# Macaron layer in fp32r on one core: x loaded one chunk ahead in the projections, and the first score maxima spread differently over their steps

## The reference

```
x = x + 0.5 * ffn(layernorm(x))
x = x + attention(layernorm(x))          # 16 heads of 32
x = x + 0.5 * ffn(layernorm(x))          # the same ffn weights

ffn(y)       = relu(y @ sign(up).T * up_scale) @ sign(down).T * down_scale * output_scale   # 2048 hidden
attention(y) = softmax(q k.T / sqrt(32)) v @ w_o.T,   q, k, v = y @ w_q.T, y @ w_k.T, y @ w_v.T
```

## Time and profile before

| | |
|---|---|
| median of 3 runs | 3113.91 us (3111.85 to 3114.26) |
| the profiled execution | 3113.91 us, span 3112.0 us |
| mean granted clock of TensorE | 0.986 |
| TensorE busy | 2973.2 us, 96% of the span |
| VectorE, ScalarE, GpSimd busy | 65%, 52%, 43% |
| projection stage | about 511 to 861 us of the span |

### The profile page before, as it was taken

How to read it: one execution, slowest core, us unless ns; L and a number is a source line. 1 busy time by engine, 2 the same in 40 slices (tenths; PEclk the granted TensorE clock), 3 DMA queues, 4 the chain that set the end, 5 groups by cost and what they waited for, 6 DMA issues and landing times.

```text
span 3112.0 us, 38839 instructions
## 1 busy us (share of the span) xinstructions
PE 2973.2 (96%) x14768; PEld 1964.9 (63%) x14768; DVE 2038.0 (65%) x3044; ACT 1613.9 (52%) x2851; POOL 1331.3 (43%) x489
## 2 busy tenths in 40 slices
PE   6999999998799999999999999999999889999998
PEld 4888887876555555555555555555555447888887
DVE  4555556766587777777787777787877234555552
ACT  5344443322166666666666666666666553333333
POOL 0000000000078787878787878788888700000000
PEclk9999999999899999999999999999999989999999
DMA  4110012563287888888888787878787754222200
GB/s 141 62 55 28 28 55 88 186 214 119 84 203 170 192 179 195 177 192 177 190 177 193 174 197 172 200 173 197 178 194 181 192 148 120 57 55 54 55 28 28
DMA packets 184891, 428.54 MB, mean 138 GB/s; under 512 B 89728, under 2 KB 90752, under 8 KB 148224
## 3 DMA queue, kind: packets, MB, share of 16 engines
q0 software_dynamic: 32400, 235.94, 32.7%
q1 hardware_dynamic: 152304, 190.11, 22.0%
HBM read 121.91 MB, written 67.63 MB: 61 GB/s over the span
## 4 chain that ended last, share of the span: by engine, by line
PE 71%; ACT 9%; DMA 6%; DVE 5%; POOL 4%; issue 4%; SPq 0%; ACTq 0%; POOLq 0%; DVEq 0%
PE bank L426 15%; PE bank L445 15%; PE bank L830 12%; PE bank L802 9%; PE bank L553 8%; ACT att_p L786 8%; PE bank L806 6%; DMA att_dma_acc<-att_p 5%; POOL att_acc L710 4%; PE bank L317 3%; DVE att_row_max L737 2%; PE bank L851 2%; PE bank L846 1%; DVE norm_inv L108 1%; ACT head_total L228 0%
## 5 line engine op out<-in xcount | busy, mean ns | idle before, releaser
L737 DVE TENSOR_REDUCE att_row_max<-bank 128x1 f32<-128x512 f32 x2048 | 1258.5, 683 | 383.5 <-PE bank L806 379.9
L786 ACT ACTIVATE att_p<-bank 128x512 f32<-128x512 f32 x2048 | 1047.0, 620 | 585.2 <-PE bank L802 573.2
L710 POOL TENSOR_TENSOR att_acc<-att_acc,att_p 128x2048 f32<-128x2048 f32 x217 | 993.4, 4578 | 222.9 <-ACT att_p L786 218.4
L802 PE MATMUL bank<-att_q,att_k 98*128 98x512 f32 x2048 | 852.7, 418 | 30.2 <-ACT att_p L786 25.6
L806 PE MATMUL bank<-att_k,att_q 96*128 96x512 f32 x2048 | 815.9, 400 | 48.8 <-DVE att_row_max L737 38.0
L802 PEld LDWEIGHTS bank<-att_q,att_k 98*128 98x128 f32 x2048 | 385.9, 189 | 403.1 <-issue 210.2
L830 PE MATMUL bank<-att_p,att_v 128*32 128x512 f32 x4096 | 502.1, 608 | 0.0
L806 PEld LDWEIGHTS bank<-att_k,att_q 96*128 96x128 f32 x2048 | 390.5, 191 | 123.6 <-DVE att_row_max L737 45.3
L369 DVE TENSOR_TENSOR ffn_hid_lo<-ffn_hid,ffn_hid_hi 128x512 fp32r<-128x512 f32 x256 | 176.1, 688 | 430.7 <-ACT ffn_hid_hi L404 412.8
L401 ACT ACTIVATE ffn_hid<-bank,up_s 128x512 f32<-128x512 f32 x256 | 176.1, 688 | 474.8 <-PE bank L426 474.2
L426 PE MATMUL bank<-hi,ffn_up_w 128*128 128x512 f32 x1024 | 402.7, 393 | 20.3 <-DVE lo L122 15.3
(11 more groups left out here) (89 smaller groups left out, 2215.9 us busy)
## 6 DMA issues: line engine op xcount, KB each, us to landing
att_dma_acc<-att_p POOLq DMA_DIRECT2D x225, 1024.0 KB, 7.6
x<-x_after_ffn SPq DMA_DIRECT2D x16, 1024.0 KB, 7.4
att_q<-q_hi SPq DMA_DIRECT2D x64, 256.0 KB, 4.2
att_k<-k_hi SPq DMA_DIRECT2D x64, 256.0 KB, 8.9
x<-xT SPq DMA_DIRECT2D x8, 1024.0 KB, 7.1
x_after_ffn<-x_out SPq DMA_DIRECT2D x8, 1024.0 KB, 9.3
q_hi<-qkv_o_hi SPq DMA_DIRECT2D x32, 256.0 KB, 2.0
q_lo<-qkv_o_lo SPq DMA_DIRECT2D x32, 256.0 KB, 2.5
```

What stands on the lines that cost most here:

```text
L710: self.nc.gpsimd.tensor_tensor(self.acc[H % 2][:], a[:], self.prob[kt % PR][:], ALU.add).then_inc(self.summed, 1)
L737: self.nc.vector.tensor_reduce(self.row_max[odd][:, qt, q:q + 1], m[:], axis=AX.X, op=ALU.max).then_inc(self.m_read, 1)
L786: self.nc.scalar.activation(self.prob[kt % PR][:, q * CH:(q + 1) * CH], self.s_ps[S_BANK[kt * QC + q]][:], ACT.Exp, scale=SCALE).then_inc( ...
L802: self.nc.tensor.matmul(self.s_ps[S_BANK[i]][:], self.k_st[H % NB][0:KM, kt * P:(kt + 1) * P], self.q_st[H % NB][0:KM, q * CH:(q + 1) * CH ...
```

## The change

It has two parts, both in the projection stage. In the steps' table, chunk 4 carries two maxima in each of steps 4 to 11 (before: steps 8 to 11), and chunks 5 and 6 one in every step (before: two in steps 0, 3, 6 and 9, one in the others). The total stays at 80, and chunk 7 keeps its 40. In SyncE's list, x of chunk n + 1 is loaded at the head of chunk n, for n from 1 to 6, where x of chunk n + 2 was loaded at the head of chunk n, for n from 0 to 5. The wait ahead of the load keeps its form.

```
-FIRST_AT = {**{(4, t): 2 for t in range(8, NT)}, **{(n, t): 1 if t % 3 else 2 for n in (5, 6) for t in range(NT)},
+FIRST_AT = {**{(4, t): 2 for t in range(4, NT)}, **{(n, t): 1 for n in (5, 6) for t in range(NT)},
             **{(7, t): 4 for t in (0, 1, 2, 3, 4, 5, 8, 9, 10, 11)}}
...
                 for n in range(NCH):
-                    if n < NCH - 2:
+                    if 1 <= n < NCH - 1:
                         sp.wait_ge(norm.dve, NV * (NCH + n + 1))
-                        st.load(sp, NCH + n + 2, x1)
+                        st.load(sp, NCH + n + 1, x1)
                     for t in range(NT):
                         qkv.store(sp, n, t)
```

## The result

| | before | after |
|---|---|---|
| median | 3113.21 us (3111.85 to 3114.26, 4 runs) | 3158.32 us (3157.16 to 3158.67, 4 runs) |
| ratio, 95% interval | | 1.0144 (1.0127 to 1.0163) |
| the profiled execution | 3113.91 us, span 3112.0 | 3161.7 us, span 3159.7 |
| projections, from chunk 1 on | 309.6 us | 352.8 us |

A forecast was written before the change was run, and what follows sets the result against it. TensorE, busy 96% of the span, was taken as the bound. Chunks 1 to 3 +22.0, chunk 4 +17.65 and +8.8, chunks 5 and 6 -5.7 sum to +42.8 us on 3113.91: 3156.7, range 3146 to 3169.

The forecast's parts named there:

- chunks 1 to 3: Projections: each chunk pays an x wait of 5.65 us and 1.7 us of lower clock, +22.0 us in all.
- chunk 4: Projections: first maximum 17.65 us later, x wait included, and +8.8 us from there to the chunk's end.
- chunks 5 and 6: Projections, twelve maxima each: 3.75 us wait goes, 4.1 us of the 6.87 stay; -2.15 and -3.55, together -5.7 us.
- The x wait: TensorE ahead of the mean product, waiting for late x: 5.65 us in chunks 1 to 4, 5.4 in 5 and 6.
- The clock: Products start further apart after a long TensorE wait: 1.7 us taken for each long wait.
- Head 0's loads: Chunk 4, step 4: first maximum waits for loads landing 19.3 us after the mean product; point reached 12.0 us later.
- The wait in step 7 of chunk 4: TensorE waits 8.4 us for row-max reductions that VectorE starts only after step 6's subtraction and norm operations.
- the small waits: Chunk 4, steps 5, 6, 8 and 9 with two maxima each: some 0.6 us apiece, 2.4 us.
- A: Rival, projections: the x wait is hidden, so chunks 1 to 3 keep their time; +5 us, or 3119; chance 0.04.
- B: Rival, projections: transfers land at once when a waiting engine leaves the queues empty; -6.1 us, or 3107.8; chance 0.02.
- C: Rival, projections: 2.45 us of clock a wait and x landing in 7.8 us; +14, 3171; chance 0.14.
- D: Rival, projections: x lands in 6.1 us and clock penalties overlap with later waits; -10, 3146; chance 0.2.

The follow-up runs named there:

- x_behind_step_6: Kernel after, but x of chunk n + 2 loaded behind the store of step 6 of chunk n: 3116.57 us, ratio 1.0014 to the kernel before.
- steps 8 and 10: Kernel after, but x of chunk n + 2 loaded behind the store of step 8 or step 10 of chunk n: 3141.09 and 3146.58 us.
- x_alone: Kernel before with only the x loads changed, the steps' table as before: 3156.08 us, ratio 1.0134.
- head_loads_early: Kernel before with the changed table, and head 0's loads moved from behind step 2 to the head of chunk 4: 3106.38 us, ratio 0.9977.

## Why the prediction was right, step by step

| term | forecast | measured |
|---|---|---|
| chunks 1 to 3 | +22.0 | +21.4 |
| chunk 4 | +26.45 | +25.5 |
| chunks 5 and 6 | -5.7 | -5.7 |
| chunk 7 | 0 | +2.0 |
| before chunk 1 and behind chunk 7, profiled execution | 0 | +4.5 |

- **The x wait, 5.65 us in chunks 1 to 4, 5.4 in 5 and 6.** Start to start (the idle and 0.16) it was 5.97, 5.30, 5.33, 5.13, 4.66 and 5.17: right, a little high. Shown by `x_behind_step_6`, which takes it away by the load's place alone, and by steps 8 and 10, where the wait followed the landing.
- **The clock, 1.7 us a wait.** Chunks 1 to 3 leave 7.34 - 5.97, 6.96 - 5.30 and 7.11 - 5.33, that is 1.4, 1.7 and 1.8 us. That the sum of these chunks came so near is in part luck: the same three chunks left 2.9, 2.4 and 2.3 us in `x_alone`. Over chunks 1 to 3 of the five profiled kernels whose x came late, a wait of 3.2 to 6.1 us drew between 1.4 and 3.0 us of lower clock, and the 3.0 stood behind the shortest of them. A wait has no fixed clock price here.
- **Head 0's loads, 12.0 us later.** Measured from the mean product (683.59) to the first maximum (701.84) it is 18.25 us where 19.3 was forecast: v landed in 7.8 us in place of 8.7. This is the largest error in chunk 4; the x wait was 0.5 us short of its forecast, and the rest of the chunk 0.7 us over. That the loads cause the wait is shown by `head_loads_early`.
- **The wait in step 7 of chunk 4, 8.4 us.** 8.23 idle, 8.39 start to start. From the first maximum to the end the chunk took 39.6 us where 38.9 was the sum, and two terms of that sum were mis-sized against each other: the small waits, 2.4 us, came to one of 0.53, and the clock, 3.4 us, to 5.2 (27 products start 0.33 us or more behind the one before without a wait, together 5.2 us over the even pace).
- **Chunks 5 and 6.** The wait of step 3 went, that of step 8 was 4.1 us start to start, as forecast. -3.1 and -2.6 stand where -2.15 and -3.55 were forecast; the sum agrees by luck. The prediction gives 0.25 us of chunk 6 to chunk 7's first step; it is chunk 6's own last maximum (799.80), which its cut at 746.70 had left out for chunk 5.
- **What was not forecast:** chunk 7 has the same list and waits as before and took 2.0 us more, with a granted clock of 0.92 where it was 0.94: behind three of its six waits of 2.01 us five to seven products in a row start at the slower pace, 18 in all, where it was two waits and 11 products. The time behind chunk 7 was 5.1 us longer in the profiled execution; over the kernels profiled here it lies between 2248.7 and 2256.4 us, in no order of the edits, so I don't put it down to the change. The timed runs, at +45.1, hold about 2 us more than the stage's 43.2.
- **Rivals.** A (x hidden) and B (transfers land at once) fall with the six waits. C and D differ from the main case in sizes only. In the changed kernel no x load at the head of chunks 1 to 6 took the 7.8 us of C or the 6.1 of D. C's dearer clock is there in `x_alone`, and D's overlap, one wait taking from the next, where the 3.75 us wait fell to 2.21. Nine of the ten long waits were within 0.8 us of their forecast, the tenth, head 0's, 1.3 us under it (8.96 us start to start against 19.3 - 7.3 - 1.7).
- By "DMA: Bandwidth & Descriptors", section "Anatomy of one DMA — SWDGE (gpsimd) path", the Trainium skill gives an estimate of 4.4 us for a 1 MB transfer, for another issue path. The traces disagree: every x load of this stage took longer, 5.7 to 8.5 us over all runs and 6.2 to 7.0 at the heads of chunks 1 to 6 of the changed kernel.

Where I was wrong was in an expectation: I took "behind the store of step 8" for a time, when it is a place in a queue.

## What to carry to other kernels

A prefetch distance is worth what the last moment allows: work out the slack of the first consumer, here 2.3 us into the chunk, and set the landing against it, with the issue time read from the queue's own rows and not from the step it is written behind. A table that spreads small products over steps should follow the free time of the engine that drains them; the nearly even spread was about 40 us slower than one that puts four where that engine is idle and none behind a long operation. When a chunk asks for data earlier, move what sends for that data too, or the gain is paid back at the first use.

## What the runs showed of the hardware that was not expected

- The same 1 MB load took 5.7 to 5.9 us to land behind step 6, in five of six cases (the sixth, just ahead of head 1's loads, 8.2), 6.2 to 7.0 at the head of a chunk in the changed kernel, behind four v stores, 6.9 to 7.8 behind step 10, with one v store after it, and 7.0 to 8.5 behind step 8, with three. That the neighbours in the queue make the difference, of up to 2.8 us, is likely but not shown: no run changes them alone.
- The same wait draws a different share of the lower clock from one time to the next: after 5.81 and 6.06 us in chunk 1, with the same lists, five and thirteen products started 0.43 us apart. What decides it these runs don't show.
- Waits of 2.01 us, six in chunk 7, don't cost the same every time: the chunk took 59.4 to 62.6 us in the eight kernels that have its list and six such waits. With the load behind step 10 (59.4 us) such a slow stretch follows one of the six, in the kernel before (60.6) two, in the changed one (62.6) three.
